# A two-layer graph network on one core: direct edges ahead of the upper half, one unit in three passes, source one-hots later

## What is computed

```python
h = relu(layernorm(x))
feat = concat([h[src], h[dst]], axis=1)
e_hh = relu(feat[:256] @ W_hh + b_hh)          # 2 tiles of 128 edges
e_oo = relu(feat[256:1536] @ W_oo + b_oo)      # 10 tiles
e_ho = relu(feat[1536:] @ W_ho + b_ho)         # 52 tiles
logit = concat([e_hh, e_oo, e_ho]) @ W_a + b_a
ex = exp(logit - segment_max(logit, dst)[dst])
alpha = ex / segment_sum(ex, dst)[dst]
z = segment_sum(alpha * h[src], dst)
nf2 = concat([h, z], axis=1)
x = x + concat([relu(nf2[:128] @ W_hn + b_hn), relu(nf2[128:] @ W_on + b_on)])
# layer 2: x = x + relu(normalised adjacency @ relu(layernorm(x)) @ W + b), with edge weights
```

## Time and profile before

| | us |
|---|---|
| median of 3 executions | 594.69 |
| lowest, highest | 589.58, 595.25 |
| the profiled execution | 592.03 |
| its span, first to last instruction | 590.1 |
| PE busy | 547.6 |
| DVE busy | 417.7 |
| ACT busy | 218.9 |
| POOL busy | 162.8 |

### The profile page before, as it was taken

One profiled execution on the slowest core, in us unless ns is written; L12 is line 12 of the kernel. 1 busy time (PEld: TensorE's weight loads), 2 busy tenths in 40 slices (PEclk: granted clock), 3 DMA queues, 4 the chain that ended last, 5 costly groups with the idle time before them and its releaser, 6 DMA issues.

```text
span 590.1 us, 7545 instructions
## 1 busy us (share of the span) xinstructions
PE 547.6 (93%) x2489; PEld 360.2 (61%) x2489; DVE 417.7 (71%) x736; ACT 218.9 (37%) x291; POOL 162.8 (28%) x163
## 2 busy tenths in 40 slices
PE   2899999999999999897899996898888999989996
PEld 2788888544444444443454464876656888868885
DVE  6999632597798889897769486746975276877234
ACT  3522445899466360020102741012534163315200
POOL 4012140477656635564564100000000001121000
PEclk9999999999999999999899995759998999999999
DMA  8956891899999999999999933040001856104002
GB/s 334 380 223 214 280 361 78 283 409 410 410 411 414 410 408 412 412 409 410 409 409 409 369 108 108 4 144 1 3 2 26 295 170 197 62 0 143 0 37 107
DMA packets 42660, 142.69 MB, mean 242 GB/s; under 512 B 5216, under 2 KB 5408, under 8 KB 42624
## 3 DMA queue, kind: packets, MB, share of 16 engines
q1 hardware_dynamic: 22000, 69.22, 31.7%
q0 software_dynamic: 19136, 69.22, 29.9%
q10 hardware_dynamic: 1488, 3.78, 1.7%
HBM read 129.60 MB, written 12.60 MB: 241 GB/s over the span
## 4 chain that ended last, share of the span: by engine, by line
PE 78%; DVE 9%; DMA 6%; issue 3%; ACT 1%; DVEq 1%; POOL 1%; ACTq 0%
PE banks L1161 24%; PE banks L1122 23%; PE banks L1211 8%; PE banks L1310 7%; PE banks L1241 6%; PE banks L1327 4%; PE banks L1259 3%; DMA w_raw<-in_L_gnn_W_on_dram 3%; DMA w_raw<-in_L_gnn_W_hn_dram 3%; DVE masked L828 1%; DVE stats L694 1%; PE banks L1275 1%; PE banks L1150 1%; PE banks L1193 1%; DVE xf L1037 1%
## 5 line engine op out<-in xcount | busy, mean ns | idle before, releaser
L452 POOL DMA_INDIRECT rows<-table,ids_i x124 | 134.3, 1083 | 136.5 <-DVE rows L793 55.1
L1161 PE MATMUL banks<-w_raw,fT_raw 128*128 128x512 f32 x384 | 166.4, 593 | 4.4 <-DMA w_raw<-in_L_gnn_W_hn_dram 2.8
L1161 PEld LDWEIGHTS banks<-w_raw,fT_raw 128*128 128x128 f32 x384 | 72.5, 190 | 96.3 <-issue 87.8
L792 DVE TENSOR_TENSOR rows<-rows 128x1024 f32<-128x1024 f32 x62 | 75.9, 1224 | 35.2 <-DMA rows<-table,ids_i 34.7
L1122 PE MATMUL banks<-w_hi,fT_hi 128*128 128x512 f32 x200 | 77.9, 389 | 0.9 <-DVE fT_lo L746 0.9
L704 DVE TENSOR_TENSOR w_lo<-w_raw,w_hi 128x1024 fp32r<-128x1024 f32 x40 | 48.2, 1221 | 41.9 <-ACT w_hi L501 41.1
L1122 PE MATMUL banks<-w_hi,fT_lo 128*128 128x512 f32 x200 | 77.8, 389 | 0.0
L1122 PE MATMUL banks<-w_lo,fT_hi 128*128 128x512 f32 x200 | 77.8, 389 | 0.0
L793 DVE SCALAR_TENSOR_TENSOR rows<-rows,wa_rep 128x1024 f32<-128x1024 f32 x62 | 75.9, 1225 | 2.1
L501 ACT ACTIVATE w_hi<-w_raw 128x1024 fp32r<-128x1024 f32 x40 | 41.5, 1055 | 78.1 <-PE banks L1122 66.3
L1241 PE MATMUL banks<-pick_src,pick_dst 128*120 x158 | 51.1, 456 | 11.6 <-DVE span_end L880 8.3
(11 more groups left out here) (169 smaller groups left out, 661.6 us busy)
## 6 DMA issues: line engine op xcount, KB each, us to landing
w_raw<-in_L_gnn_W_ho_dram SPq DMA_DIRECT2D x16, 512.0 KB, 6.4
table<-stage SPq DMA_DIRECT2D x32, 256.0 KB, 6.5
w_raw<-in_L_gnn_W_oo_dram SPq DMA_DIRECT2D x16, 512.0 KB, 7.0
w_raw<-in_L_gnn_W_on_dram SPq DMA_DIRECT2D x16, 512.0 KB, 6.4
w_raw<-in_L_gnn_W_hn_dram SPq DMA_DIRECT2D x16, 512.0 KB, 6.2
w_raw<-in_L_gnn_W_hh_dram SPq DMA_DIRECT2D x16, 512.0 KB, 6.8
w_raw<-in_L_gnn_W_dram SPq DMA_DIRECT2D x8, 512.0 KB, 4.4
xf<-in_x_dram SPq DMA_DIRECT2D x4, 512.0 KB, 5.1
```

The costliest lines, as they stand in the source:

```text
L452: pool.indirect_dma_start(out=rows[:, slot, side, :], out_offset=None, in_=table[kind][side], in_offset=bass.IndirectOffsetOnAxis(ap=ids_i ...
L792: step(dve.tensor_tensor(rows[:, r, 0, :], rows[:, r, 0, :], rows[:, r, 1, :], ALU.add))
L1161: ins = pe.matmul(bank[j][:, :], fT_raw[:, k, m * P:(m + 1) * P], w_raw[:, c % SLOTS, n * H:(n + 1) * H], start=(k == 0), stop=(k == K - 1))
```

## The change

Five things are moved.

1. **Unit 2 in three passes.** `RAW` begins with unit 3, so unit 2 is made with `chunk()`, and gets `hi` and `lo` for its 8 chunks. `whole_features` moves from unit 1 to unit 3 (c = 25 to 28), one call of two slices each.
2. **HH before TOP.** PE's order is unit 3, HH, TOP with 2 banks, TOP with 6 banks. The transposed direct-edge features are copied back into `h_edge` and not into `fT_raw`; HH uses banks 4 to 7. Weight chunks are loaded in the new order.
3. **Places in the lists of ACT and DVE.** In ACT's loop `keep_edges(0)` stands at c = 50, `keep_edges(1)` at 52, TOP's first two banks at 55; `FIRST_SRC` is 28. In DVE's loop `hh_edges` stands at c = 49, `evacuate(1)` ahead of `lo(19)`. The lifts that PE spreads stand behind other chunks.
4. **Memory.** `pick_src` lies over `h_edge`, `fT_lo`, `w_hi` and `w_lo`; the one-hots of odd spans lie over `fT_hi` and wait for the end of TOP. The first span is made after DVE's loop.
5. **Tiny products among spans.** The degrees are made in 16 parts behind spans 1 to 4 and 10 to 21, the node maxima in 4 parts behind spans 6 to 9. The last chunk's maxima move from span 4 to 5 of DVE's list, the exponents from 6 to 10, their split from 8 to 12.

```diff
-    C_TOP = K * UNITS
-    C_HH = C_TOP + 2 * K
-    C_BOT = C_HH + 2 * K
+    C_HH = K * UNITS
+    C_TOP = C_HH + 2 * K
+    C_BOT = C_TOP + 2 * K
...
-    RAW = range(2 * K, C_BOT)
+    RAW = range(3 * K, C_BOT)
...
-        BY_PE = {3: (C_TOP + 4, 0), 4: (C_TOP + K + 4, 6), 5: (C_HH + 4, 6), 6: (C_HH + 13, 4)}
-        LAST_MAX, ME_PE, ME_DVE, PARTS, EXP = 4, 4, 6, 8, 4
-        FIRST_SRC, EARLY_SRC = 17, 3 * T // 8
+        BY_PE = {3: (C_HH + 6, 2), 4: (C_HH + 13, 2), 5: (C_TOP + K + 1, 0), 6: (C_TOP + K + 6, 0)}
+        HH_BANK = 4
+        LAST_MAX, ME_PE, ME_DVE, PARTS, EXP = 5, range(6, 10), 10, 12, 10
+        DEG_PE = (*range(1, 5), *range(10, 22))
+        FIRST_SRC, EARLY_SRC = 28, 3 * T // 8
...
 (keep_edges, ACT)
-                    act.activation(fT_raw[:, 2 * g:2 * g + 2, side * 2 * P:(side + 1) * 2 * P],
-                                   bank[4 + g % 2].rearrange("p (f e) -> p f e", f=2), ACT.Copy).then_inc(hh_raw_done, 1)
+                    act.activation(h_edge[:, side, :, 2 * g * P:2 * (g + 1) * P],
+                                   bank[g % 2 if side else g].rearrange("p (f e) -> p f e", f=2), ACT.Copy).then_inc(hh_raw_done, 1)
 (pick, ACT)
                 if n == 0:
-                    act.wait_ge(chunk_used, 2 * K)
+                    act.wait_ge(chunk_used, 3 * K)
...
-                    act.wait_ge(chunk_used, C_HH + K + pair + 1)
+                    act.wait_ge(hh_logits, TILE_HH)
 (loop of ACT)
             for c in range(4, C_BOT):
-                if c == C_TOP + 10:
+                if c == 50:
+                    keep_edges(0)
+                if c == 52:
+                    keep_edges(1)
+                if c == 55:
                     for s in range(STAGE):
                         act.wait_ge(stored[s], 16 * UNITS)
-                    keep_top(range(2, 8))
-                if c == C_TOP + 14:
                     keep_top(range(2))
-                if c == C_HH + 4:
-                    act.wait_ge(chunk_used, C_HH)
-                    keep_edges(0)
-                if c == C_HH + 8:
-                    keep_edges(1)
...
             for pair in range(EARLY_SRC, T // 2):
                 pick(pair)
-            act.wait_ge(hh_logits, TILE_HH)
+            keep_top(LAST_TOP)
             act.wait_ge(edge_done, TE)
 (loop of DVE)
             for c in range(4, C_BOT):
+                if c == 19:
+                    evacuate(1)
...
-                if c == C_BOT - 1:
+                if c == 49:
                     hh_edges()
-                    dve.wait_ge(hh_logits, TILE_HH)
-                    spread(0, w_col)
...
-                if c in (17, 18):
-                    whole_features(2 * (c - 17))
+                if c in (25, 26, 27, 28):
+                    whole_features(2 * (c - 25))
...
-            for n in range(1, SPANS):
+            for n in range(SPANS):
                 spread(n, w_col)
 (list of PE)
+            for k in range(K):
+                chunk(2 * K + k, k, k % 4, ALL, 8)
...
-            for u in range(2, UNITS):
+            for u in range(3, UNITS):
...
+            transpose_edges(0)
...
             for k in range(2 * K):
                 if k == K - 2:
                     transpose_edges(1)
...
+            for k in range(K):
+                raw_chunk(C_TOP + k, k, range(2), None)
+            pe.wait_ge(hh_logits, TILE_HH)
+            pe.wait_ge(max_done, B * 5)
+            for k in range(K):
+                raw_chunk(C_TOP + K + k, k, LAST_TOP, None)
+                spread_lifts(C_TOP + K + k)
...
-                if n == ME_PE:
-                    degrees(range(T // 4), closes=True)
-                if n == ME_PE:
-                    node_maxima()
+                if n in DEG_PE:
+                    part = DEG_PE.index(n)
+                    degrees(range(4 * part, 4 * part + 4), part == 0, part == len(DEG_PE) - 1)
+                if n in ME_PE:
+                    node_maxima(ME_PE.index(n))
```

More of the change, by code:

```diff
@@ L88, in chunk_rows @@
             q, k = (c - (C_BOT if bottom else C_TOP)) // K, c % K
[L89 removed]
+            w, row = (W_on if q else W_hn), bottom * D + k * P
         else:
@@ L144, in build @@
         tail = rows_at + ROWS * 2 * D * 4 - 2 * B * N * 4
-        pick_dst = [sb(f"pick_dst{r}", [P, T, 3, SPAN], BF16, over=base)[0] for r, base in enumerate((tail, at))]
+        pick_dst = [sb(f"pick_dst{r}", [P, T, 3, SPAN], BF16, over=base)[0] for r, base in enumerate((tail, fT_at))]
         wa_rep, at = sb("wa_rep", [P, D], F32)
@@ L255, in bank_ready @@
             elif unit == TOP:
-                if j in (1, 7):
-                    eng.wait_ge(chunk_used, first + (2 * K if j == 1 else K))
+                if j in (1, LAST_TOP[-1]):
+                    eng.wait_ge(chunk_used, first + (K if j == 1 else 2 * K))
                 else:
-                    eng.wait_ge(bank_done, before + (j - 1 if j > 1 else 6))
+                    eng.wait_ge(bank_done, before + (2 + LAST_TOP.index(j) if j else 1))
             elif j == (3 if unit == HH else 7):
@@ L641, in _ @@
                 keep_span(SPANS + n)
+                if SPANS + n == DEG_PE[-1] + 1:
+                    act.wait_ge(deg_done, 1)
+                    act.activation(sums[:, :, :], bank[6][:, 0:4 * B].rearrange("p (b k) -> p b k", k=4), ACT.Copy).then_inc(sums_out, 1)
                 if n % 2 == 1 and n < 2 * B:
@@ L1152, in spread_lifts, with raw_chunk @@
                         ins.then_inc(lift_full, 1)
-            def raw_chunk(c, k, banks, evac_wait=8 * UNITS - 8):
+            for k in range(K):
+                chunk(2 * K + k, k, k % 4, ALL, 8)
+            def raw_chunk(c, k, banks, evac_wait):
                 pe.wait_ge(w_in[c % SLOTS], 16 * (c // SLOTS + 1))
                 for j in banks:
-                    if k == 0:
+                    if k == 0 and evac_wait is not None:
                         pe.wait_ge(evac, evac_wait + j + 1)
@@ L1268, in fold_span, with node_maxima @@
                               start=True, stop=True).then_inc(rows_summed, 1)
-            def node_maxima():
+            def node_maxima(part):
                 pe.wait_ge(mpart_ready, 1)
-                for t in range(T):
+                for t in range(part * T // len(ME_PE), (part + 1) * T // len(ME_PE)):
                     for b in range(B):
```

77 lines of the change are left out of this document (31 added, 46 removed).

## The result

The changed kernel takes **622.70 us** (median of 5 runs, 618.78 to 622.87) beside 593.23 us for the kernel before on the same chip (5 runs, 589.58 to 595.25): a ratio of 1.0498, with the 95% interval 1.0459 to 1.0537. It is slower, as forecast, and inside the range, but by 5.0% and not by the 2% of the forecast.

What follows compares the result with a forecast made beforehand. TensorE is busy 93% of 590.1 us, but DMA and VectorE run nearly together with it from 106 to 161 us. Span stage from 372, plus 92.4, ends 15.8 us later: 592.0 + 15.8 = 607.8, stated as 607 us, range 593 to 624.

Steps and rivals of the forecast that it cites:

- Unit 2 in three passes: TensorE in unit 2: 11.3 us less work, unit 2 ending at 149.6, the saving ending at unit 3's evacuation.
- Tiny products among spans: Span stage: degree and node-maximum parts between spans, 84.4 us from span 0 at full clock, 92.4 taken with half clock.
- They are hidden: Unit 2: 8 added hi copies on ACT and 8 lo subtractions on DVE are covered; uncovered, the subtractions cost 9.8 us.
- The wait for the copies: Before the direct edges: TensorE idles 26 us, 213 to 239.2, for ACT's copy behind 14 pairs of one-hots.
- Rival A: ACT's direct-edge copy comes when TensorE needs it; last lift at 344, time 574 to 583 us; chance 0.16.
- What waits behind: After the late copies: DVE waits 26 us for chunk 3, last lift at 369.5, span stage starts at 372.
- The two waits in it that no row showed: DVE before the last lift: about 2 us for the second lift spread, some 2.5 for gathers contending with weights.
- The fall of the clock behind span 5: Span stage: clock falls in the wait behind span 5, stays half over spans 6 to 9, adding 8 us.
- 3 x 2.6 and 2 us behind DVE's split: Span stage, spans 10 to 12: three spans at 2.6 us plus a 2 us wait for DVE, 9.8 us.
- The sum: Whole kernel: span stage ends at 464.4 instead of 448.6, 15.8 us later; 592.0 + 15.8 = 607.8 us.
- D: Rival: clock stays half far into the span stage's second round, 19 us over ten more spans, 625 us; chance 0.08.

Runs made afterwards that it cites:

- e4: The changed kernel with unit 2 made of whole float32 products again and whole features back in unit 1: 617.97 us, ratio 1.0426.
- e12: e9 with DVE's whole_features calls at c = 23, 24, 25, 27 instead of 25 to 28: 587.32 us, ratio 0.9915.
- e7: e6 with unit 2 made of whole float32 products again: 590.01 us, ratio 0.9969.
- e1: The changed kernel with the two direct-edge copies (keep_edges) at c = 39 and 47 instead of 50 and 52: 602.57 us, ratio 1.0162.
- e3: The changed kernel with both direct-edge copies (keep_edges) at c = 54 instead of 50 and 52: 625.05 us, ratio 1.0535.
- e6: e5 with all 256 degree products in one run ahead of span 0 and none between spans: 590.99 us, ratio 0.9986.
- e8: The kernel before with only degrees in 16 parts, node maxima in 4, and later last maxima, exponents, split and Exp: 604.69 us, ratio 1.0249.
- e5: e1 with node maxima in one block at span 4, and last maxima, exponents and split where they were before: 599.20 us, ratio 1.0132.
- e9: e6 with evacuate(2) ahead of the first lift's send, evacuate(3) at c = 34, copies at c = 38 and 46: 591.51 us, ratio 0.9947.
- e10: The kernel before with unit 2 in three passes, FIRST_SRC = 28, later whole_features, first direct-edge copy at c = 47: 595.41 us, ratio 1.0045.

## Why the prediction was right and where it was too small

The direction and the chain of causes were right; two steps failed. The tiny products among spans were taken as nearly neutral (1.7 us), and the runs put them at 11.6 and 11.8 us; inside that term, spans 10 to 12 took 15.5 us and not 9.8. And "They are hidden", said of unit 2's added work, did not hold: fetch 2, on which the copies hang, went out 3.4 us later.

*Unit 2 in three passes: right on TensorE, wrong that the rest is hidden.* Unit 2 ended at 149.95 (forecast 149.6). But "They are hidden" failed. The lift 0 of DVE came at 148.49 instead of 143.25, the evacuation and the first `whole_features` behind it, so TensorE waited 5.94 us and ran the first 3.7 us of unit 3 at half clock: it ended at 212.9, not at 206. In this kernel that cost little, as DVE emptied the banks only from 210.2 to 215.1 and TensorE then stood for 28 us. What cost was that fetch 2 went out at 206.05 and not at 202.7, and everything hung on it. e4 puts the price at 4.7 us, with the reservation above. With the copies in time and both late calls moved (e12, 587.32), the three passes are not shown to bring anything either: e7, without them, has 590.01, the two ratios' intervals overlap, and e12's other moves were not tried on a kernel like e7.

*The wait for the copies: the mechanism and nearly the size.* Forecast: TensorE idle for 26 us, first product at 239.2, HH to 302. Measured: 27.97 us, 242.63, 306.5. The 14 pairs took 35.5 us (14 x 2.54 = 35.6); the 3.4 us of difference are fetch 2's. e1 to e3 confirm that the place of the copies decides, one for one from c = 44 on. Rival A is close to e1, in time as the rival wanted (copy at 215.26). It came to 602.6 us in the changed kernel's frame and not to 574 to 583: A was mis-sized by about 20 us at the least (15 by the profiled execution, 598.22), because the last lift then comes at 354.3 and not at 344, with DVE's edges late behind its evacuation and `hh_edges`, and because the span stage took 97.4 us and not 84 to 92.

*What waits behind.* DVE waited 31.3 us for chunk 3 (forecast 26: it arrived at 242.5 and was released at 273.87 instead of 269.3), `hh_edges` was done at 309.2 (305.3), the last lift ready at 375.17 (369.5), 66.0 us later where the sum had 64.2. (The parts that the sum names make 63.7 and so 369.0. The two waits in it that no row showed, 2 us for the second spread and 2.5 for gathers, measured 2.7 and 3.5.) Span 0 started at 378.31, the forecast said 372. Of those 6.3 us, 3.4 are the copies, 0.5 the block of HH up to the end of `hh_edges`, 1.8 DVE's rest and 0.6 the hand-over.

*Tiny products among spans: the mis-sized term.* Forecast 92.4 us from span 0, measured 97.1, part by part:

| part | forecast | measured |
|---|---|---|
| spans 0 and 1 | 5.2 | 4.4 |
| spans 2 to 5 | 10.4 | 12.3 |
| wait for DVE | 4.5 | 4.3 |
| spans 6 to 9 | 23.6 | 21.8 |
| spans 10 to 12 | 9.8 | 15.5 |
| spans 13 to 25 | 38.8 | 38.8 |

The fall of the clock behind span 5 came as forecast, at 398.6, and cost less than the 8 us taken: spans 6 to 9 took 21.8 us where the forecast had 15.6 at full clock. It came in two stretches, to 402.0 and again from 405.4 to 419.1; span 7 began between them at full clock. Spans 2 to 5 took 2.92 us each and not 2.6: the products of a span 1.68, its folds 0.82, a part of the degrees 0.42 (386.25 to 389.17). The step that failed most is "3 x 2.6 and 2 us behind DVE's split". It left out that the exponents stand behind the *last* part of the node maxima. The timeline of DVE:

```profile
421.29 0.36 DVE L948 TENSOR_REDUCE me<-banks 128x64 f32<-128x192 f32 x1 [6.63 <-PE banks L1276]
...
427.38 0.19 DVE L735 CAST part<-ex 128x64 bf16<-128x64 f32 x1
```

DVE stood idle for 6.63 us until the fourth part was done at 421.1. Span 11's one-hots, whose buffer was free when span 9's products ended at 418.6, stand behind that wait in DVE's list and began at 422.25. TensorE then ran out of them, waited 1.84 us before 426.09 and was at half clock from 425.9 to 429.3. Cutting the node maxima into four parts thus puts off what hangs on the last one: it stands three spans behind the first (419.50 and 402.75).

A second error is hidden in that sum. 92.4 from span 0 is only 1.7 us more than before (88.1 from span 1, and 2.6 for a span), so the forecast held this part of the change nearly neutral. e6 and e8 put it at 11.6 and 11.8 us. The kernel before had 39.3 us of half clock in this stage, the changed one 23.7, so the stages' lengths alone (97.1 us and the 90.7 by which the forecast counts the one before) understate it. The rows of before held the warning: the 192 degree products filled a gap, which the prediction says, and it then added their price without asking for a cover.

*The sum.* The forecast was 11.0 us under the profiled execution: 6.3 at span 0 and 4.7 in the stage. Another 3.9 us is that the profiled execution is the lowest of its five runs, and 0.8 the rounding of 607.8 down. So the time fell into the upper end of the range, which the prediction had given to D, a slow clock in the second round. That was not what happened: spans 13 to 25 took the 38.8 us of the forecast. (D's own terms add to 626.8 us and not to 625.)

*Where the 29 us went*, by medians: 20.1 are the place of the copies (changed kernel to e1), 11.6 the tiny products among spans (e1 to e6); with both taken back 590.99 us remain beside 592.85, a ratio whose interval includes 1. Direct edges ahead of the upper half are by themselves neither a gain nor a loss that these runs resolve. The most that any version here gave, with the copies, the tiny products, both evacuations and `whole_features` standing elsewhere, is e12's 0.9%.

## What to carry to other kernels

When work is taken from the busiest engine, look up where each hand-over to the next stage comes from, and count what the other engines have to do more for it: here 11.3 us of saved products came to nothing or to a loss (4.7 us by the medians) in each pair of versions that differed by them. In a list that runs in order, place a short copy that another engine waits for ahead of bulk work that nobody waits for yet; here that was two numbers, and 20 us. Tiny products belong where the engine waits anyway (8.2 us here). A sum cut into parts among other work delays its consumer to the last part: the trace shows the wait, but e5 did not show that one block is faster.

## What the runs showed of the hardware

**A wait of 6 us at the hand-over of two dense stages costs clock as well.** In the stage from 149.95 to 212.9 the granted clock is 0.95; in the changed kernel the stretch from 152.8 to 159.6, the second half of the wait and the first products after it, was at half clock:

```profile
152.80:159.60 6.80, 3.72 (x5) 1.67 (x6) 6.73 (x8) 4.46 (x10) 5.58 (x5) 0.50 1.03 411
```

Unit 3 took 57.03 us for 128 records, against 54.9 at full clock by the earlier trace rows (64 x 0.858) and 55.09 in e12, where the wait is gone and with it the half clock there. The Trainium skill ("TensorE: Matmul & The Clock Gate", What's actually happening) has the half clock as the default state from which activity releases the engine, and the trace agrees.

**A weight load behind the stores of a table lands 12 to 15 us after its issue, with DMA as full as elsewhere.** In e6, as in e9, TensorE waited in the middle of the direct edges for weights (4.5 us). The list of SP, and what the trace has of the four loads of 512 KB issued from 222.9 to 233.2:

```profile
213.01 4.07 SPq L382 DMA_DIRECT2D table<-stage  x8
222.88 10.63 SPq L360 DMA_DIRECT2D w_raw<-in_L_gnn_W_hh_dram  x4
```

```profile
  DMA w_raw<-in_L_gnn_W_hh_dram: 4.5, 1
...
DMA to landing us min/median/max: 12.0/13.3/14.6
```

The gathers alone don't explain it. The four loads issued from 192.0 to 212.6, ahead of the stores, land in 6.8 to 8.2 us, and those at 243.1 and 246.5 in 6.8 and 6.7, all while DMA moves 408 to 411 GB/s (414 to 419 around the late ones). What sets the late four apart is the eight stores of 256 KB just ahead of them from the same engine, which themselves land in 9 to 15 us. No run moves the stores alone, so this cause is argued and not shown. The fit in the Trainium skill ("DMA: Bandwidth & Descriptors", Anatomy of one DMA), 2.0 us and bytes at 436 GB/s, is for GpSimd's transfers, each by itself; for 512 KB it gives an estimate of 3.2 us, and these loads, issued by SP beside gathers, take twice that and more. A buffer of four chunks that are used in 3.43 us each covers 13.7 us: enough for the landing times of 7 to 8 us, and no longer for 14.6.

**The same kernel spreads by up to 10 us.** e7's runs go from 586.03 to 595.44, e9's from 585.10 to 594.23. In the profiled executions the half-clock stretches of the span stage fall in different places and make 21 us (e12) to 46 us (e10) of it. The ratios of versions with 4 runs have intervals of 0.7% to 1.2% to either side, those with 10 or 12 runs 0.35% to 0.5%: a difference of 1% in this kernel needs a dozen runs.
